# Two-layer conditional kernel: low parts and weight sums moved from GpSimd to VectorE

## The chip, the cores and the metric

One core of a Trainium2 chip runs the kernel. The metric is the device time of one execution in microseconds. The times shown are the median of three runs; the profile is that of one more execution, recorded by the hardware profiler.

## What is computed

The input x is 16 batches of 512 tokens by 512 features in f32. Each batch has a language id and an expert id.

```python
h = relu(x @ w1[language] + b1[language])                       # 512 -> 128
adapted = h @ w2[language] + b2[language]                       # 128 -> 512
x1 = x + layernorm(x + adapted) * gamma[language] + beta[language]
g = gelu(x1 @ W1 + B1)                                          # 512 -> 2048, exact gelu
out = x1 + concat([g @ W2 + B2, g @ We[expert] + be[expert]])   # 384 + 128 columns
```

## The kernel before

The batches are worked on in eight pairs. Within a pair the hidden width of 2048 is cut into eight groups (k = 0 to 7) of 2 x 128 columns. All operands of TensorE (PE) are split: a high part, rounded to the type fp32r by ScalarE (ACT), and a low part, which is the value minus its high part. Every product of two matrices is three matmuls, high by high, high by low and low by high (lines 276 to 278; line numbers are those of the profile). A 128x512 low part is one TENSOR_TENSOR subtraction on VectorE (DVE) or GpSimd (POOL).

**The up product.** For the two batches of a pair and the two halves of the inner dimension, the blocks B11, B21, B12, B22 of x1 and A11, A12, A21, A22 of the weights are multiplied in Strassen's way with seven products instead of eight, P1 to P7, into the banks up_a, up_b and up_c. The products need sums of blocks, T1 to T4 (128x512 in two halves c each), and sums of weights, S1 to S4 (128x256 each). T1 = B12 - B11, T2 = B22 - T1, T3 = B22 - B12, T4 = B21 - T2. P5 needs T1, P6 needs T2, P7 needs T3 and P4 needs T4, in the order P1, P5, P6, P2, P3, P7, P4 (`pe_step`). P2 needs B21 and P3 needs B22. VectorE makes the values of T (`dve_t1` to `dve_t4`), ScalarE rounds them (`act_t_hi`), and the low part is made by GpSimd (`pool_t_lo`, line 1362), but for T1 of the second pair, which is `dve_t_lo` (line 1029).

**The first pair.** Its weights come raw from memory. For each group k from 1 the sums S1 to S4 are made by GpSimd (`pool_weight_sums`, lines 1369 to 1377), ScalarE rounds all seven weight blocks (`act_w1_hi`, line 751) and VectorE makes their low part (`dve_w1_lo`, line 1060). Both parts are kept in device memory and loaded again by the later pairs (`keep_w1`, `load_w1`).

**The other work.** While PE works on pair i, the adapter of pair i + 1 is worked on in between: its weights are split (`act_aw_hi`, then `pool_aw_lo`, line 1284, or in one place `dve_aw_lo`, line 1073), its products go to PE (`pe_adapter_up` into aux; `pe_adapter_down` in groups 2 to 5, the first token tile into up_a, the second into up_c), and VectorE does the layer norm. The down product (`pe_down`, 24 matmuls for one batch and group) reads g from VectorE (`dve_g_lo`, line 876) and expert weights from GpSimd (`pool_expert`, lines 1356 and 1358). VectorE adds the finished banks to the output (`dve_down_sum`: eight small operations for batch 0, lines 888 and 890; four for batch 1, line 895). GpSimd also makes the residual (`pool_residual`, line 1339) and two sums per token tile of the next pair (`pool_biases`, lines 1296 and 1298).

**The order.** Each engine's order is written out by hand, by `pe_step`, `act_step`, `dve_step`, `pool_step` and `sp_pair` and their branches for the first pair. An engine takes its instructions strictly in that order and waits on semaphores. The second half of the adapter's down product may not write up_c before VectorE has read the group's P5 and P3 out of it:

```python
pe_adapter_down(eng, m, b, t, up_a)
eng.wait_ge(dve_c12, seven(i, k + 1))      # dve_sum_c12, line 866
pe_adapter_down(eng, m, b, t + 1, up_c)
```

The down product of batch 1 at a pair's end waits for the sum of batch 0 (`dve_out[0]`), and the next x may be loaded only when the T and B blocks that share its buffer have been read:

```python
if b == 0 and k < 2 and m is not pairs[1]:
    eng.wait_ge(b_low, m.count(6, 0))
    eng.wait_ge(dve_t, m.count(8, 0))      # all of T1 to T4 made
```

## Time and profile before

| | |
|---|---|
| median of 3 runs | 1426.03 us (1424.87 to 1427.23) |
| profiled execution | 1425.13 us, its span 1423.3 us |
| PE busy | 1413.5 us, 99% of the span |
| VectorE busy | 892.8 us, 63% |
| GpSimd busy | 648.2 us, 46% |
| ScalarE busy | 588.8 us, 41% |
| granted clock of PE, mean | 0.999 |

In a row of the timeline the first number is the start in us from the span's start and the second is the time from the start of the row's first instruction to the end of its last. An instruction's own duration overlaps the next one's start, so the spacing of starts is a little shorter than the duration. In brackets stands the idle time of the engine ahead of the row and what ended it. A granted clock of 1.00 is 2.4 GHz, one of 0.50 is 1.2 GHz; in a row of the windows it stands third from the end, behind the length of the stretch and the busy time of PE, its weight load, VectorE, ScalarE and GpSimd, and ahead of the DMA share and GB/s.

### The profile page before, as it was taken

What the parts mean: (1) busy time and instruction counts of PE and PEld (TensorE: products, weight loads), DVE (VectorE), ACT (ScalarE), POOL (GpSimd) and SP (SyncE); (2) the same over time, 40 slices, a digit from 0 to 9 for tenths busy, and PEclk for the clock granted to TensorE, in tenths of its full rate; (3) what the DMA queues carried; (4) which work ended last, traced back from release to release, by engine and by line L of the source; (5) the groups of instructions that cost most, each with busy time, mean ns of one, the idle gap of its engine ahead of it and who ended that gap; (6) DMA issues with size and microseconds to landing.
All of it is one profiled execution on the core that took longest, in us unless ns stands there. A gap on an engine that the chain in (4) does not pass through costs nothing.

```text
span 1423.3 us, 18598 instructions
## 1 busy us (share of the span) xinstructions
PE 1413.5 (99%) x6220; PEld 1162.7 (82%) x6220; DVE 892.8 (63%) x1457; ACT 588.8 (41%) x968; POOL 648.2 (46%) x643
## 2 busy tenths in 40 slices
PE   9999999999999999999999999999999999999999
PEld 6788878888888888888888888888888888888887
DVE  6998794765746756568566575556666576643333
ACT  4844454333543335343353434443345333533231
POOL 5996365451464424734257342563335633351101
PEclk9999999999999999999999999999999999999999
DMA  8646897457765677566774677646876458654332
GB/s 270 251 158 220 227 365 252 168 177 201 253 227 181 188 220 249 197 215 172 228 255 161 211 191 242 240 152 200 226 246 244 147 176 222 199 193 163 134 111 89
DMA packets 273955, 292.37 MB, mean 205 GB/s; under 512 B 129602, under 2 KB 230722, under 8 KB 265796
## 3 DMA queue, kind: packets, MB, share of 16 engines
q1 hardware_dynamic: 264068, 188.15, 44.3%
q10 hardware_dynamic: 9792, 103.03, 19.1%
q8 instruction: 50, 0.82, 0.2%
q14 instruction: 45, 0.37, 0.1%
HBM read 238.70 MB, written 52.43 MB: 205 GB/s over the span
## 4 chain that ended last, share of the span: by engine, by line
PE 93%; SPq 2%; DVE 2%; issue 1%; DMA 1%; POOL 1%; ACT 0%; DVEq 0%; ACTq 0%
PE down L277 16%; PE down L276 16%; PE down L278 16%; PE up_b L277 5%; PE up_b L278 5%; PE up_b L276 5%; PE up_c L277 4%; PE up_c L278 4%; PE up_c L276 4%; PE up_a L277 4%; PE up_a L278 4%; PE up_a L276 4%; SPq L1627 1%; PE aux L276 1%; PE aux L278 1%
## 5 line engine op out<-in xcount | busy, mean ns | idle before, releaser
L876 DVE TENSOR_TENSOR g<-g_raw,g 128x512 fp32r<-128x512 f32 x256 | 231.3, 932 | 280.3 <-ACT g L663 280.3
L277 PE MATMUL down<-w,g 128*128 128x512 f32 x1024 | 398.4, 389 | 0.0
L276 PE MATMUL down<-w,g 128*128 128x512 f32 x1024 | 398.4, 389 | 0.0
L278 PE MATMUL down<-w,g 128*128 128x512 f32 x1024 | 398.3, 389 | 0.0
L1356 POOL CAST w<-w_raw 128x256 fp32r<-128x256 f32 x125 | 72.1, 577 | 526.6 <-DMA w_raw<-m_we 526.6
L277 PEld LDWEIGHTS down<-w,g 128*128 128x128 f32 x1024 | 192.3, 188 | 40.0
L278 PEld LDWEIGHTS down<-w,g 128*128 128x128 f32 x1024 | 192.3, 188 | 39.9
L276 PEld LDWEIGHTS down<-w,g 128*128 128x128 f32 x1024 | 192.1, 188 | 40.0
L637 ACT COPY u<-up_b 128x512 f32<-128x512 f32 x63 | 37.1, 589 | 309.0 <-PE up_b L278 289.3
L663 ACT CAST g<-g_raw 128x512 fp32r<-128x512 f32 x256 | 159.0, 621 | 8.1
L655 ACT ACTIVATE g_raw<-u,m_b_sb 128x512 f32<-128x512 f32 x63 | 45.6, 723 | 229.5 <-PE down L278 217.2
L276 PE MATMUL up_b<-bo,w 128*128 128x512 f32 x336 | 130.8, 389 | 1.1 <-POOL bo L1362 1.1
L278 PE MATMUL up_b<-bo,w 128*128 128x512 f32 x336 | 130.7, 389 | 0.0
L277 PE MATMUL up_b<-bo,w 128*128 128x512 f32 x336 | 130.7, 389 | 0.0
L1358 POOL TENSOR_TENSOR w<-w_raw,w 128x256 fp32r<-128x256 f32 x128 | 113.2, 884 | 10.0
L895 DVE TENSOR_TENSOR resid<-down,resid 128x512 f32<-128x512 f32 x128 | 83.5, 684 | 41.8 <-PE down L278 41.8
L655 ACT ACTIVATE g_raw<-up_b,m_b_sb 128x512 f32<-128x512 f32 x63 | 43.2, 686 | 139.7 <-PE up_b L278 139.6
L1339 POOL TENSOR_TENSOR resid<-x,m_bias 128x512 f32<-128x512 f32 x64 | 89.7, 1432 | 0.0
L276 PE MATMUL up_c<-bo,w 128*128 128x512 f32 x224 | 87.1, 389 | 0.0
L277 PE MATMUL up_c<-bo,w 128*128 128x512 f32 x224 | 87.1, 389 | 0.0
L278 PE MATMUL up_c<-bo,w 128*128 128x512 f32 x224 | 87.1, 389 | 0.0
L866 DVE TENSOR_TENSOR u<-up_c,u 128x512 f32<-128x512 f32 x63 | 43.4, 689 | 62.0 <-PE up_c L278 53.9
(224 smaller groups left out, 2443.1 us busy)
## 6 DMA issues: line engine op xcount, KB each, us to landing
w<-w_kept ACTq DMA_DIRECT2D x55, 1792.0 KB, 7.6
w<-w_kept SPq DMA_DIRECT2D x56, 768.0 KB, 4.9
w_raw<-m_we SPq DMA_DIRECT2D x128, 128.0 KB, 4.6
out<-resid SPq DMA_DIRECT2D x64, 256.0 KB, 4.4
xTs_raw<-xT SPq DMA_DIRECT2D x56, 256.0 KB, 3.1
xs<-x SPq DMA_DIRECT2D x56, 256.0 KB, 6.5
w_kept<-w SPq DMA_DIRECT2D x8, 1792.0 KB, 8.9
x_turned<-turned SPq DMA_DIRECT2D x112, 128.0 KB, 3.5
```

The lines of the kernel that those rows point to most:

```text
L276: eng.matmul(bank, a_hi, b_hi, start=opens, stop=False, skip_group_check=True)
L277: eng.matmul(bank, a_hi, b_lo, start=False, stop=False, skip_group_check=True)
L278: return eng.matmul(bank, a_lo, b_hi, start=False, stop=closes, skip_group_check=True)
L637: eng.copy(u2[:, :], up_b[:, :]).then_inc(act_u2, 1)
L655: eng.activation(values, source, ACT.Gelu, bias=m_b1_sb[:, j:j + 1]).then_inc(act_gelu, 1)
L663: eng.copy(g[:, b, k % 2, h, HI, :], values).then_inc(act_ghi[b], 1)
L866: eng.tensor_tensor(u2[:, :], up_c[:, :], u2[:, :], ALU.add).then_inc(dve_c12, 1)
L876: eng.tensor_tensor(g[:, b, k % 2, h, LO, :], g_raw[:, b, k % 2, h, LO, :], raw(g[:, b, k % 2, h, HI, :]), ALU.subtract).then_inc(dve_glo[ ...
L895: eng.tensor_tensor(resid[:, 1, t, :], down[t][:, :], resid[:, 1, t, :], ALU.add).then_inc(dve_out[1], 1)
L1339: eng.tensor_tensor(resid[:, b, t, :], x1[:, b, t, :], m_bias[:, b, :], ALU.add).then_inc(pool_res, 1)
L1356: eng.tensor_copy(hi, values).then_inc(pool_eh[b], 1)
L1358: eng.tensor_tensor(lo, values, raw(hi), ALU.subtract).then_inc(pool_e[b], 1)
```

## The change

VectorE gets the weight sums of groups 2 to 7 of the first pair (`dve_weight_sums`); GpSimd keeps those of group 1 and of the group loaded again at the pair's end. VectorE gets the low parts of T2 and T3 of the first pair and of all four T of every later pair; GpSimd keeps T1 and T4 of the first pair. VectorE gets all adapter weights' low parts in later pairs, and the first of the first pair. One semaphore per T takes the place of a common one. On ScalarE the rounding of B22 goes ahead of that of T3, and T4's behind the gelu of C11. At the very start of the program PE corrects each half of B11 directly behind its first products, and ScalarE keeps each half directly behind its rounding.

```diff
+        if k in (1, GROUPS):
+            eng.wait_ge(pool_s, 4 * (1 + k // GROUPS))
+        else:
+            eng.wait_ge(dve_s, 4 * (k - 1))
         eng.copy(w1[:, k % 2, HI, :, :], w1_raw[:, k % 2, LO, :, :]).then_inc(act_w1hi, 1)
 
     def act_w2_hi(eng, k):
...
+    def dve_weight_sums(eng, k):
+
+        w, n = w1_raw[:, k % 2, LO], 4 * (k - 2)
+        eng.wait_ge(in_w1raw[k % 2], 48 * (k // 2 + 1))
+        eng.tensor_tensor(w[:, S1, :], a21[:, k % 2, :], w[:, A22, :], ALU.add).then_inc(dve_s, 1)
+        eng.tensor_tensor(w[:, S3, :], w[:, A11, :], a21[:, k % 2, :], ALU.subtract).then_inc(dve_s, 1)
+        eng.wait_ge(dve_s, n + 1)
+        eng.tensor_tensor(w[:, S2, :], w[:, S1, :], w[:, A11, :], ALU.subtract).then_inc(dve_s, 1)
+        eng.wait_ge(dve_s, n + 3)
+        eng.tensor_tensor(w[:, S4, :], w[:, A12, :], w[:, S2, :], ALU.subtract).then_inc(dve_s, 1)
+
     def dve_w1_lo(eng, k):
         eng.wait_ge(act_w1hi, k)
...
@@ -1075,6 +1091,7 @@
     def dve_second_step(eng, i, m):
 
         dve_g_lo(eng, i, 0, C11)
+        dve_weight_sums(eng, 2)
         dve_g_lo(eng, i, 0, C21)
         dve_first_t4(eng, 0)
         dve_first_t4(eng, 1)
@@ -1121,11 +1138,14 @@
             dve_g_lo(eng, i, 6, C22)
         if k == 2:
             dve_g_lo(eng, i, 0, C22)
+            dve_weight_sums(eng, 3)
             dve_sum_c12(eng, i, k)
         if k % 2 == 0:
             dve_down_sum(eng, i, 0, k - 1)
         else:
             dve_down_sum(eng, i, 1, k - 2)
+        if 2 < k < GROUPS - 1:
+            dve_weight_sums(eng, k + 1)
         if k == GROUPS - 1:
             for c in range(2):
                 dve_t1(eng, m, c)
@@ -1182,14 +1202,19 @@
     def dve_next_blocks(eng, i):
 
         for c in range(2):
-            dve_t3(eng, i, c)
+            dve_t_lo(eng, i, T2, c)
         if before(i) is first:
             for c in range(2):
                 dve_b_lo(eng, i, B21, c)
         for c in range(2):
-            dve_t4(eng, i, c)
+            dve_t3(eng, i, c)
         for c in range(2):
             dve_b_lo(eng, i, B22, c)
...
+        for c in range(2):
+            dve_t_lo(eng, i, T3, c)
+        dve_down_sum(eng, before(i), 0, GROUPS - 1)
+        for c in range(2):
+            dve_t4(eng, i, c)
 
     def dve_step(eng, i, m, k):
         if i is first:
@@ -1205,7 +1230,6 @@
             dve_g_lo(eng, before(i), GROUPS - 1, C21)
         if k == 0:
             dve_next_blocks(eng, i)
-            dve_down_sum(eng, before(i), 0, GROUPS - 1)
         if m and last:
             for c in range(2):
                 dve_b_lo(eng, m, B11, c)
@@ -1216,6 +1240,10 @@
                 b, c = ADAPTER_UP[k]
                 dve_xT_lo(eng, m, b, c)
                 dve_xT_lo(eng, m, b, c + 1)
+            if k == 2:
+                dve_aw_lo(eng, m, 1, 0)
+            if k == 4:
+                dve_aw_lo(eng, m, 1, 1)
         if k == 1 or k > 2:
             dve_g_lo(eng, i, k - 1, C12)
             dve_g_lo(eng, i, k - 1, C22)
@@ -1246,14 +1274,19 @@
         if m and k == 1:
             dve_xT_lo(eng, m, 0, 2)
             dve_xT_lo(eng, m, 0, 3)
+            dve_aw_lo(eng, m, 0, 1)
         if m and last:
             for c in range(2):
                 dve_t1(eng, m, c)
         if not (m and k in (4, 5)):
             dve_sum_c12(eng, i, k)
         dve_sum_c22(eng, i, k)
+        if k == 0:
+            for c in range(2):
+                dve_t_lo(eng, i, T4, c)
         dve_g_lo(eng, i, k, C11)
         if m and k == 0:
+            dve_aw_lo(eng, m, 0, 0)
             dve_xT_lo(eng, m, 0, 0)
             dve_xT_lo(eng, m, 0, 1)
         if k == 0:
@@ -1269,6 +1302,8 @@
             dve_turns(eng, m, 0, 0)
         if m and last:
             for c in range(2):
+                dve_t_lo(eng, m, T1, c)
+            for c in range(2):
                 dve_t2(eng, m, c)
             for c in range(2):
...
-            for of in (T1, T2):
-                for c in range(2):
-                    pool_t_lo(eng, i, of, c)
-            pool_t_lo(eng, i, T3, 0)
-            pool_aw_lo(eng, m, 0, 0)
-            pool_t_lo(eng, i, T3, 1)
+            for c in range(2):
+                pool_t_lo(eng, i, T1, c)
             return
         if k == 1:
-            pool_weight_sums(eng, 2)
             pool_t_lo(eng, i, T4, 0)
             pool_t_lo(eng, i, T4, 1)
             pool_expert(eng, i, 0, 1)
+            eng.wait_ge(aw_split, m.front(4, 1))
             pool_aw_lo(eng, m, 0, 1)
...
@@ -1447,15 +1470,6 @@
         if i is first:
             pool_first_step(eng, i, m, k)
             return
-        if k == 0:
-            pool_t_lo(eng, i, T3, 0)
-            pool_t_lo(eng, i, T3, 1)
-            if before(i) is first:
-                pool_aw_lo(eng, m, 0, 0)
-            pool_t_lo(eng, i, T4, 0)
-            pool_t_lo(eng, i, T4, 1)
-            if m and before(i) is not first:
-                pool_aw_lo(eng, m, 0, 0)
         if m:
             pool_roots(eng, m, k)
         if k % 2 == 1:
@@ -1463,33 +1477,22 @@
             pool_expert(eng, i, 1, k - 1)
         elif k > 0:
             pool_expert(eng, i, 1, k - 1)
-        if m and k == 2:
-            pool_aw_lo(eng, m, 1, 0)
         if k in (1, 2):
             for t in range(TT):
                 pool_residual(eng, i, k - 1, t)
...
@@ -1956,10 +1957,15 @@
                 dve_b_lo(eng, first, B22, c, FIRST_B22[c])
             dve_w1_lo(eng, 1)
             for c in range(2):
+                dve_t_lo(eng, first, T2, c)
+            for c in range(2):
                 dve_t3(eng, first, c, FIRST_B22[c])
+            dve_xT_lo(eng, pairs[1], 0, 0)
+            dve_aw_lo(eng, pairs[1], 0, 0)
+            dve_xT_lo(eng, pairs[1], 0, 1)
+            for c in range(2):
+                dve_t_lo(eng, first, T3, c)
             dve_w2_lo(eng, 0)
-            for c in range(2):
-                dve_xT_lo(eng, pairs[1], 0, c)
             run(eng, dve_step)
             dve_g_lo(eng, last_pair, GROUPS - 1, C21)
             dve_down_sum(eng, last_pair, 0, GROUPS - 1)
```

What is left out: the semaphores' names, the body of the sums (now the same on both engines, with the engine's own semaphore), the moved rounding on ScalarE, and GpSimd's low parts in the first pair's groups 0 and 7.

Three places show the new order. The first is VectorE in group 2 of the first pair, ahead of the sum that reads up_c (u<-up_c). Before (aw is the adapter's weight, g the gelu's output, u the sum):

```order
L1073 TENSOR_TENSOR aw<-aw_raw,aw 128x512 [waits aw_split,aw_rounded]
L876 TENSOR_TENSOR g<-g_raw,g 128x512 [waits act_ghi1]
L866 TENSOR_TENSOR u_66<-up_c,u_66 128x512 [waits act_u2,pe_p3]
L888 TENSOR_TENSOR resid<-down,resid 128x128 [waits pool_res,pe_y0]
L890 TENSOR_TENSOR resid<-down,resid 128x384
```

Now:

```order
L1089 TENSOR_TENSOR aw<-aw_raw,aw 128x512 [waits aw_split,aw_rounded]
L881 TENSOR_TENSOR g<-g_raw,g 128x512 [waits act_ghi1]
L1067 TENSOR_TENSOR w_raw<-a_73,w_raw 128x256 [waits in_w1raw_1]
L1068 TENSOR_TENSOR w_raw<-w_raw,a_73 128x256
L1070 TENSOR_TENSOR w_raw<-w_raw 128x256 [waits dve_s]
L1072 TENSOR_TENSOR w_raw<-w_raw 128x256 [waits dve_s]
L871 TENSOR_TENSOR u_66<-up_c,u_66 128x512 [waits act_u2,pe_p3]
L893 TENSOR_TENSOR resid<-down,resid 128x128 [waits pool_res,pe_y0]
```

The four weight sums of group 3 (w_raw) have come between g and the sum that reads up_c.

The second place is GpSimd in groups 1 and 2 of the first pair. Before (bo is T4's low part, w_51 an expert's, aw an adapter's, x_68 and xs the sums for the next pair, w_raw the weight sums):

```order
L1362 TENSOR_TENSOR bo<-bo_raw,bo 128x512 [waits act_thi] x2
L1358 TENSOR_TENSOR w_51<-w_raw,w_51 128x2x128 [waits act_eh0,in_e0_1]
L1284 TENSOR_TENSOR aw<-aw_raw,aw 128x512 [waits aw_rounded]
L1339 TENSOR_TENSOR resid<-x_68,m_bias 128x512 [waits in_mb0,dve_x1] x4
L1296 TENSOR_TENSOR x_68<-xs,vecs 128x512 [waits pool_res,pe_tr0,in_vec0,in_x0_0]
L1298 TENSOR_TENSOR xs<-xs,vecs 128x512 [waits pool_xb]
L1358 TENSOR_TENSOR w_51<-w_raw,w_51 128x2x128 [waits act_eh1,in_e1_0]
L1369 TENSOR_TENSOR w_raw<-a_73,w_raw 128x256 [waits in_w1raw_1]
L1371 TENSOR_TENSOR w_raw<-w_raw,a_73 128x256
L1374 TENSOR_TENSOR w_raw<-w_raw 128x256 [waits pool_s]
L1377 TENSOR_TENSOR w_raw<-w_raw 128x256 [waits pool_s]
L1296 TENSOR_TENSOR x_68<-xs,vecs 128x512 [waits in_x0_1]
```

Now:

```order
L1397 TENSOR_TENSOR bo<-bo_raw,bo 128x512 [waits act_thi] x2
L1393 TENSOR_TENSOR w_51<-w_raw,w_51 128x2x128 [waits act_eh0,in_e0_1]
L1319 TENSOR_TENSOR aw<-aw_raw,aw 128x512 [waits aw_rounded,aw_split]
L1374 TENSOR_TENSOR resid<-x_68,m_bias 128x512 [waits in_mb0,dve_x1] x4
L1331 TENSOR_TENSOR x_68<-xs,vecs 128x512 [waits pool_res,pe_tr0,in_vec0,in_x0_0]
L1333 TENSOR_TENSOR xs<-xs,vecs 128x512 [waits pool_xb]
L1393 TENSOR_TENSOR w_51<-w_raw,w_51 128x2x128 [waits act_eh1,in_e1_0]
L1331 TENSOR_TENSOR x_68<-xs,vecs 128x512 [waits in_x0_1]
L1333 TENSOR_TENSOR xs<-xs,vecs 128x512 [waits pool_xb]
L1393 TENSOR_TENSOR w_51<-w_raw,w_51 128x2x128 [waits act_eh1,in_e1_1]
```

The sums for the next pair follow each other with one expert's low part in between; the weight sums are gone.

The third place is VectorE from the first pair's end into group 0 of the second pair. Before (h_raw is T2, the first bo_raw T3, the second T4; bo<-xTs_raw the low parts of B21, then of B22; resid<-down the output sums of batch 0):

```order
L876 TENSOR_TENSOR g<-g_raw,g 128x512 [waits act_ghi0]
L1040 TENSOR_TENSOR bo_raw<-xTs_raw,b_64 128x512 [waits pe_p7,in_turned1_2]
L1040 TENSOR_TENSOR bo_raw<-xTs_raw,b_64 128x512 [waits pe_p7,in_turned1_3]
L1001 TENSOR_TENSOR bo<-xTs_raw,bo 128x512 [waits act_bhi] x2
L1056 TENSOR_TENSOR bo_raw<-xTs_raw,h_raw 128x512 [waits dve_t,pe_p4,in_turned0_2]
L1056 TENSOR_TENSOR bo_raw<-xTs_raw,h_raw 128x512 [waits dve_t,pe_p4,in_turned0_3]
L1001 TENSOR_TENSOR bo<-xTs_raw,bo 128x512 [waits act_bhi] x2
L888 TENSOR_TENSOR resid<-down,resid 128x128 [waits dve_out0,pe_y0]
L890 TENSOR_TENSOR resid<-down,resid 128x384
```

Now:

```order
L881 TENSOR_TENSOR g<-g_raw,g 128x512 [waits act_ghi0]
L1034 TENSOR_TENSOR bo<-h_raw,bo 128x512 [waits act_thi] x2
L1006 TENSOR_TENSOR bo<-xTs_raw,bo 128x512 [waits act_bhi] x2
L1045 TENSOR_TENSOR bo_raw<-xTs_raw,b_64 128x512 [waits pe_p7,in_turned1_2]
L1045 TENSOR_TENSOR bo_raw<-xTs_raw,b_64 128x512 [waits pe_p7,in_turned1_3]
L1006 TENSOR_TENSOR bo<-xTs_raw,bo 128x512 [waits act_bhi] x2
L1034 TENSOR_TENSOR bo<-bo_raw,bo 128x512 [waits act_thi] x2
L893 TENSOR_TENSOR resid<-down,resid 128x128 [waits dve_out0,pe_y0]
L895 TENSOR_TENSOR resid<-down,resid 128x384
```

T2's low part (bo<-h_raw) and T3's (bo<-bo_raw) have come in. B21's low part has moved ahead of T3, B22's ahead of the making of T4, and the eight output sums, of which the last two rows are the first, now also stand ahead of T4.

## Rows read from the trace of the kernel before

**Rows 1.** the page's engine totals: busy us, share of the span, instructions
```profile
PE 1413.5 (99%) x6220; PEld 1162.7 (82%) x6220; DVE 892.8 (63%) x1457; ACT 588.8 (41%) x968; POOL 648.2 (46%) x643
```

**Rows 2.** waits of PE, whole program: us in total, times, longest
```profile
PE up_c L339 <- DVE bo L1001: 2.6, 2, 1.5
PE up_b L276 <- POOL bo L1362: 1.1, 1, 1.1
PE aux L276 <- POOL aw L1284: 0.4, 1, 0.4
```

**Rows 3.** timeline of VectorE, 60 to 75 us: start us, us from start to end of the row
```profile
60.50 5.18 DVE L876 TENSOR_TENSOR g<-g_raw,g 128x512 fp32r<-128x512 f32 x3
72.39 1.23 DVE L876 TENSOR_TENSOR g<-g_raw,g 128x512 fp32r<-128x512 f32 x1
73.55 0.67 DVE L866 TENSOR_TENSOR u<-up_c,u 128x512 f32<-128x512 f32 x1
74.15 0.27 DVE L888 TENSOR_TENSOR resid<-down,resid 128x128 f32<-128x128 f32 x1
74.35 0.54 DVE L890 TENSOR_TENSOR resid<-down,resid 128x384 f32<-128x384 f32 x1
```

**Rows 4.** timeline of GpSimd, 61 to 78 us
```profile
61.70 6.83 POOL L1339 TENSOR_TENSOR resid<-x,m_bias 128x512 f32<-128x512 f32 x4
76.40 1.29 POOL L1296 TENSOR_TENSOR x<-xs,vecs 128x512 f32<-128x512 f32 x1
```

**Rows 5.** timeline of PE at 76 us: second half of the adapter's down product
```profile
75.96 0.39 PE L276 MATMUL up_c<-aw,h 128*128 128x512 f32 x1
```

**Rows 6.** timeline of VectorE at 119 us, of GpSimd at 120 us
```profile
119.00 0.69 DVE L866 TENSOR_TENSOR u<-up_c,u 128x512 f32<-128x512 f32 x1 [1.56 <-PE up_c L278]
...
120.49 1.29 POOL L1296 TENSOR_TENSOR x<-xs,vecs 128x512 f32<-128x512 f32 x1
```

**Rows 7.** timeline of PE, 201 to 210 us, then the clock in a stretch of it
```profile
201.31 0.99 PE L339 MATMUL up_a<-bo,w 128*128 128x512 f32 x2
202.83 0.40 PE L332 MATMUL up_c<-bo,w 128*128 128x512 f32 x1
206.38 0.80 PE L339 MATMUL up_c<-bo,w 128*128 128x512 f32 x1 [1.18 <-DVE bo L1001]
209.47 0.40 PE L276 MATMUL down<-w,g 128*128 128x512 f32 x1
...
206.00:209.00 3.00, 2.62 (x6) 2.13 (x7) 3.00 (x10) 0.00 (x0) 1.47 (x1) 0.50 0.92 372
```

**Rows 8.** timeline of VectorE, 194 to 207 us
```profile
194.86 3.48 DVE L1040 TENSOR_TENSOR bo_raw<-xTs_raw,b 128x512 f32<-128x512 f32 x2
198.26 3.48 DVE L1001 TENSOR_TENSOR bo<-xTs_raw,bo 128x512 fp32r<-128x512 f32 x2
203.97 2.36 DVE L1001 TENSOR_TENSOR bo<-xTs_raw,bo 128x512 fp32r<-128x512 f32 x2
```

**Rows 9.** timeline: the next pair's x, its DMA issue, rounding and first product
```profile
206.40 1.06 SPq L1503 DMA_DIRECT2D xTs_raw<-xT  x2
...
213.81 1.27 ACT L668 CAST xTs<-xTs_raw 128x512 fp32r<-128x512 f32 x2 [7.87 <-DMA xTs_raw<-xT]
...
219.03 0.39 PE L276 MATMUL aux<-xTs,aw 128*128 128x512 f32 x1
```

**Rows 10.** timeline of GpSimd, VectorE and PE, third pair, group 2, 418 to 430 us
```profile
421.30 5.93 POOL L1339 TENSOR_TENSOR resid<-x,m_bias 128x512 f32<-128x512 f32 x4
...
418.90 1.29 DVE L901 TENSOR_TENSOR xTs<-xTs_raw,xTs 128x512 fp32r<-128x512 f32 x2
422.76 3.33 DVE L876 TENSOR_TENSOR g<-g_raw,g 128x512 fp32r<-128x512 f32 x2
426.01 0.68 DVE L866 TENSOR_TENSOR u<-up_c,u 128x512 f32<-128x512 f32 x1
...
429.15 0.39 PE L276 MATMUL up_c<-aw,h 128*128 128x512 f32 x1
```

More of the change, by code:

```diff
@@ L813, in act_step @@
             for c in range(2):
+                act_block_hi(eng, i, B22, c)
+            for c in range(2):
                 act_t_hi(eng, i, T3, c)
-            for c in range(2):
-                act_block_hi(eng, i, B22, c)
             if before(i) is first:
@@ L1440, in pool_first_step @@
             pool_expert(eng, i, 1, k)
-            for of, c in T_ORDER[2:4]:
-                pool_t_lo(eng, m, of, c)
         elif k % 2 == 1:
@@ L1489, in pool_step @@
             pool_expert(eng, i, 1, k)
-            if m:
-                for of, c in T_ORDER[2:4]:
-                    pool_t_lo(eng, m, of, c)
     def load_xT(eng, m, b, k):
@@ L1640, in load_blocks @@
             eng.wait_ge(dve_t, m.count(8, 0))
-            eng.wait_ge(pool_tlo, m.count(8, 0))
+            eng.wait_ge(t_low[T1], m.count(2, 0))
         else:
@@ L1843, in _ @@
                 first_hi(eng, C11, A11, B11, c, c == 0)
-            for c in range(2):
                 pe_first_low(eng, B11, c, FIRST_B11[c])
@@ L1900, in _ @@
                 act_first_hi(eng, B11, c, FIRST_B11[c])
-            for c in range(2):
                 act_first_keep(eng, B11, c, FIRST_B11[c])
@@ L1958, in _ @@
             for c in range(2):
+                dve_t_lo(eng, first, T2, c)
+            for c in range(2):
                 dve_t3(eng, first, c, FIRST_B22[c])
+            dve_xT_lo(eng, pairs[1], 0, 0)
+            dve_aw_lo(eng, pairs[1], 0, 0)
+            dve_xT_lo(eng, pairs[1], 0, 1)
+            for c in range(2):
+                dve_t_lo(eng, first, T3, c)
             dve_w2_lo(eng, 0)
-            for c in range(2):
-                dve_xT_lo(eng, pairs[1], 0, c)
             run(eng, dve_step)
```

49 lines of the change are left out of this document (18 added, 31 removed).

## The prediction

> **What bounds the kernel now.** I read the engine totals first: PE is busy for 1413.5 of 1423.3 us [rows 1]. A VectorE or GpSimd instruction is therefore worth only what it makes PE wait. Next come the waits of PE; the ones that this change can touch are 2.6 us on VectorE's low part of B22, in two waits, 1.1 us on T2's low part by GpSimd and 0.4 us on an adapter weight's low part by GpSimd [rows 2]. All lie in the first pair or at the boundary to the second. So at most about 5 us are to be had, and the timelines of VectorE and GpSimd must then say whether VectorE, with more to do, comes late somewhere else.
>
> **The price of a shared stretch.** The change moves work between two engines that slow each other. Three low parts of 128x512 take 5.18 us where GpSimd is busy, 1.70 us each counted from start to start, and one takes some 0.60 alone (two in 1.29, the second's tail included) [rows 3, 10]. GpSimd's operation of the same size takes 1.29 alone and 1.70 in company (four in 6.83) [rows 4]. So where both have a queue they alternate: one of each in 1.70 us, of which 0.60 are VectorE's own and 1.10 go to GpSimd. The sum of up_c, which reads PSUM, takes 0.67 beside a busy GpSimd [rows 3] and isn't slowed. A 128x256 sum on VectorE does not occur before. By the 128- and 384-wide rows, 0.27 and 0.54 long with the tail [rows 3], I estimate 0.33 us of its own; beside a GpSimd that has a 512-wide operation ready each time it would be 0.33 + 1.10 = 1.43 us. The Trainium skill ("SBUF — State Buffer", "SBUF: two separate sides") says that the port pair is locked for a whole instruction and the other engine fully blocks: by that a sum would be 0.33 + 1.29 = 1.62. The trace is a little kinder, 1.70 where the rule would have 1.89 for a pair of 512-wide ones, and I go by the trace.
>
> **Start of the program.** T2's low part comes from VectorE right behind T2 and the 1.1 us wait goes [rows 2]; B11's corrections in another order save perhaps 0.2. But ScalarE has another rounding ahead, so P6 moves little; the adapter's wait of 0.4 goes. In all PE is about 0.5 us (0 to 1.5) earlier afterwards. It gains nothing at the end, because the next stall is set by VectorE and swallows it: 0.
>
> **Group 2 of the first pair.** The sum of up_c starts at 73.55 and ends at 74.22 [rows 3]; the second half of the adapter's down product, which waits for it, would start at 75.96 [rows 5]. Slack is 1.74 us. The change puts four weight sums ahead of this sum. VectorE also gets there about 0.5 us later, at 74.05, because of group 2's sums and two low parts earlier (estimate). GpSimd, which has residuals, the sums for the next pair and experts' low parts queued in a row, has work all through, so most of the four sums meet one of its operations. Alone they would cost 4 x 0.33 = 1.3 us, with each contended 4 x 1.43 = 5.7. Some of GpSimd's operations are only 256 wide, so I take 1.25 each, 5.0 us, near the upper end, as the g ahead of them is contended too (1.16 to the next start instead of some 0.60 [rows 3]). The sum of up_c then ends at 79.7 and PE goes on at 79.8: **+3.85** (0 to +5). Nothing follows on PE that could be taken forward: its order is strict.
>
> **The clock behind that wait.** At the pair boundary PE idled for 1.47 and 1.18 us, and then ran at a granted clock of 0.50, the 1.2 GHz level, until about 209: matmuls lasted 0.80 and not 0.39 [rows 7]. From 206.38 to 209.47 are 3.1 us, half of which is lost. A stall of almost 4 us should bring the same: **+1.5** (0 to 2).
>
> **Groups 3 to 6.** Here the sums stand behind the down product's sums. In group 4 the sum of up_c starts at 119.00 with VectorE idle for 1.56 ahead of it, and GpSimd begins its sums for the next pair beside it at 120.49 [rows 6]; those now come earlier. The sums of groups 5 and 6 are done beside them. Slack there is 1.2 us, and 4 x 1.43 = 5.7 does not fit quite: **+0.6** for both (0 to 2). In groups 3 and 6 VectorE's idle time covers them: 0. If that cover were gone, each late sum would be passed on 1 to 1.
>
> **The boundary to the second pair.** Before, VectorE made T3 (3.48 us for two), B21's low part (3.48), T4, and B22's low part at 203.97 (2.36) [rows 8]. PE needed the last at 203.05, right behind 202.83, and waited; with the clock behind it and 0.4 us for B21's low part (0.99 instead of 0.61 for two at 201.31) the down product of group 7 began at 209.47 [rows 7]. Without waits it is 204.48, 14 matmuls behind 201.31 at 0.227 us each (1413.5 / 6220 [rows 1]). Now GpSimd has nothing at this place, so VectorE runs at 0.60: T2's low part 194.9 to 196.1, B21's to 197.3, T3 to 198.5, B22's to 199.7, T3's low to 200.9. The eight output sums (0.20 and 0.46 us apart, 2.65 us [rows 3]) end at 203.5, T4 at 204.7. All stand before their use: **-5.0** (-5.3 to -4). What becomes late next: the next pair's x is loaded behind the last reader of its buffer. It was issued at 206.40 and its rounding waited 7.87 us, till 213.81, for a transfer beside full queues (DMA share 0.92 [rows 7, 9]). Its first product ran at 219.03 [rows 9] and without the 5.0 us it comes at 214.0. The issue comes only 1.6 us earlier, and the load lands no earlier, as the queues are full; rounding and low part follow, to 215.1. So **+1.0** (0 to 2) comes back.
>
> **Second to seventh pair, group 2.** This repeats six times. In the third pair the adapter's down product is at 429.15; up_c is summed at 426.01 to 426.69, with slack 2.4 [rows 10]. The change puts a low part of an adapter weight ahead (0.60 alone, 1.70 contended), and GpSimd, rid of its own, starts its four residuals (5.93 [rows 10]) earlier, so more of VectorE's operations fall beside it: one or two at 1.10 each. I get the sum's end at 429.2 against 429.15, **+0.1** each, **+0.6** (0 to +9). One more GpSimd operation in that stretch gives another 1.1 each, 6.6 in all. T1 and T2 at the pair's end, and T4 in group 0, have idle VectorE time around them: 0.
>
> **Sum.** 3.85 + 1.5 + 0.6 - 5.0 + 1.0 + 0.6 = +2.55 on the profiled execution's 1425.13, 1427.7. The median of the runs is 0.9 above that execution, so **1428.5 us**. That is within 0.2% (2.85 us, about what a measurement of this kernel can tell from no change), but near its upper edge.
>
> **Rivals.**
> - *VectorE keeps the port.* The four sums are short and follow at once, and GpSimd may not get in between. Then they cost 1.3 to 1.8 us, the stall in group 2 is 0.2 to 0.7 and the clock stays up. For it: g at 72.39 took 1.23, not 1.70 [rows 3]. Against: three g in a row alternated at 1.70. The Trainium skill (same section) gives the pair to whichever instruction starts first, which this rival would fit as well; who goes first when both wait it doesn't say. The sum becomes 0.5 + 0 + 0.2 - 5.0 + 1.0 + 0 = -3.3, 1422.7 us: faster. Chance 0.2.
> - *The wait repeats in six pairs (slower).* The adapter weight's low part in group 2 meets one more GpSimd residual than I count. The end of up_c's sum passes 429.15 by 1.1 us in each, and PE waits six times. It decides from one operation on, as the slack left is about 0. Added to the forecast it is +6.6, 1435 us. For it: 2.4 us of slack against 1.7 for the low part and 1.1 for another. Against: GpSimd may have done its residuals before VectorE's own work there begins. Chance 0.15.
> - *The boundary wait is only moved.* x's load lands or B22's rounding comes late, so that two stalls of over a microsecond stay and the clock falls again: -2 in place of -4, some 1431 us. Chance 0.13. It needs ScalarE to be late with the B22 and T3 roundings, which it now does first.
>
> **How the numbers follow.** The forecast's own case has 0.52; its unknown costs (0 to 5, 0 to 2, 0 to 2) make it 1424.5 to 1431.5. Faster by over 0.2% needs under 1423.2: the first rival. Slower needs over 1428.9: the two slow rivals, 0.28, and somewhat under half of the forecast's case, which lies just beside that edge. So 0.2, 0.35, 0.45. The range from 1421.8 to 1433.5 takes in the first rival, the third and the forecast, and leaves the second's upper part out.
>
> **What would show it.** Right: a PE wait of 3 to 4 us on up_c near 76 us, released by VectorE's sum, with the clock at 0.50 behind it; VectorE's four sums spaced about 1.25 us; no wait of L339's at 203 us, and one of about 1 us at the adapter's up product near 214. Wrong: sums at 0.33 us, or no drop of the clock behind the wait; PE waits in group 2 of later pairs; a wait at the boundary on B22 or T3.

## The result and the profile after

The changed kernel takes **1429.11 us** (median of 14 runs, 1426.26 to 1430.42), the kernel before in the same runs 1426.27 us (14 runs, 1423.56 to 1428.24). The ratio is 1.0020, with a 95% interval from 1.0012 to 1.0027: slower by 0.2%, 2.84 us by the medians. The profiled execution took 1428.87 us, its span is 1427.1, against 1425.13 and 1423.3 before.

| PE reaches the same matmul at | before | after | difference | change since the row above |
|---|---|---|---|---|
| down product, group 1 of the first pair | 63.04 | 63.13 | +0.09 | +0.09 |
| adapter's down product in up_c, group 2 | 75.96 | 79.02 | +3.06 | +2.97 |
| up product of group 3, past the slow clock | 82.08 | 86.65 | +4.57 | +1.51 |
| down product of group 7 at the pair boundary | 209.47 | 209.05 | -0.42 | -4.99 |
| adapter's up product, second pair | 219.03 | 219.95 | +0.92 | +1.34 |
| adapter's down product in up_c, second pair, group 2 | 255.07 | 257.04 | +1.97 | +1.05 |
| last matmul | 1419.68 | 1423.41 | +3.73 | +1.76 |

The table is made from the timelines of PE. The page's engine totals and the waits of PE (us in total, times, longest):

```profile
PE 1414.9 (99%) x6220; PEld 1163.5 (82%) x6220; DVE 926.3 (65%) x1564; ACT 589.9 (41%) x968; POOL 514.1 (36%) x536
...
PE up_c L277 <- DVE u L871: 3.5, 2, 2.7
...
PE up_b L277 <- ACT up_b L630: 1.5, 1, 1.5
PE aux L277 <- DVE xTs L906: 1.2, 1, 1.2
PE down L277 <- DVE g L881: 0.5, 1, 0.5
```

GpSimd has 134 us less to do than before, VectorE 33.5 us more, and PE is as full [rows 1]. The two waits on B22 and the ones on GpSimd [rows 2] are gone. In their place stand waits on VectorE's sum of up_c, on ScalarE's copy into up_b in the first pair, on x's low part and, 0.5 us, on g. VectorE in the stretch of [rows 3], where the four weight sums are the L1067 to L1072 rows and L871 is the sum of up_c:

```profile
73.16 1.51 DVE L1067 TENSOR_TENSOR w_raw<-a,w_raw 128x256 f32<-128x256 f32 x1
74.59 1.51 DVE L1068 TENSOR_TENSOR w_raw<-w_raw,a 128x256 f32<-128x256 f32 x1
76.02 0.94 DVE L1070 TENSOR_TENSOR w_raw<-w_raw 128x256 f32<-128x256 f32 x1
77.00 1.37 DVE L1072 TENSOR_TENSOR w_raw<-w_raw 128x256 f32<-128x256 f32 x1
78.29 0.68 DVE L871 TENSOR_TENSOR u<-up_c,u 128x512 f32<-128x512 f32 x1
```

GpSimd in the same stretch (compare [rows 4]), with no idle time:

```profile
72.65 1.73 POOL L1331 TENSOR_TENSOR x<-xs,vecs 128x512 f32<-128x512 f32 x1
74.46 1.35 POOL L1333 TENSOR_TENSOR xs<-xs,vecs 128x512 f32<-128x512 f32 x1
75.78 0.91 POOL L1393 TENSOR_TENSOR w<-w_raw,w 128x256 fp32r<-128x256 f32 x1
76.64 1.44 POOL L1331 TENSOR_TENSOR x<-xs,vecs 128x512 f32<-128x512 f32 x1
```

The first two sums and the fourth stand beside 512-wide operations of GpSimd, the third, the shortest, beside the 256-wide one that began at 75.78: from start to start they take 1.43, 1.43, 0.98 and 1.29 us, 5.13 in all. PE there (compare [rows 5]), and the clock behind the wait:

```profile
79.02 0.79 PE L277 MATMUL up_c<-aw,h 128*128 128x512 f32 x1 [2.69 <-DVE u L871]
80.47 0.63 PE L277 MATMUL down<-w,g 128*128 128x512 f32 x1
...
79.00:82.00 3.00, 2.98 (x7) 2.40 (x8) 3.00 (x9) 1.09 (x1) 2.92 (x3) 0.50 0.00 0
```

PE is idle for 2.69 us ahead of the needed sum's reader, and then six matmuls and more run at the granted clock of 0.50, which is 1.2 GHz. At the boundary GpSimd has no instruction from 197.7 until past 212, so VectorE is not slowed by it (compare [rows 8]):

```profile
199.19 1.30 DVE L1034 TENSOR_TENSOR bo<-h_raw,bo 128x512 fp32r<-128x512 f32 x2 [0.34 <-ACT bo L748]
200.40 1.28 DVE L1006 TENSOR_TENSOR bo<-xTs_raw,bo 128x512 fp32r<-128x512 f32 x2
201.60 1.28 DVE L1045 TENSOR_TENSOR bo_raw<-xTs_raw,b 128x512 f32<-128x512 f32 x2
202.81 1.29 DVE L1006 TENSOR_TENSOR bo<-xTs_raw,bo 128x512 fp32r<-128x512 f32 x2
204.01 1.29 DVE L1034 TENSOR_TENSOR bo<-bo_raw,bo 128x512 fp32r<-128x512 f32 x2
...
207.86 1.29 DVE L1061 TENSOR_TENSOR bo_raw<-xTs_raw,h_raw 128x512 f32<-128x512 f32 x2
```

In order: T2's low part, B21's, T3, B22's, T3's low part and, behind the output sums, T4. Ten operations take 0.60 us each where they took up to 1.70. B22's low part is done at 204.1. PE, which needed it at once before, needs it at 207.24 here:

```profile
207.24 0.62 PE L340 MATMUL up_c<-bo,w 128*128 128x512 f32 x2
...
209.05 0.39 PE L277 MATMUL down<-w,g 128*128 128x512 f32 x1
```

Behind it the next x is late (compare [rows 9]); first its DMA issue, then ScalarE, then PE:

```profile
211.26 1.02 SPq L1506 DMA_DIRECT2D xTs_raw<-xT  x2
...
218.46 1.24 ACT L669 CAST xTs<-xTs_raw 128x512 fp32r<-128x512 f32 x2 [8.65 <-DMA xTs_raw<-xT]
...
219.95 0.47 PE L277 MATMUL aux<-xTs,aw 128*128 128x512 f32 x1 [1.22 <-DVE xTs L906]
```

And this is group 2 of the third pair (compare [rows 10]):

```profile
415.89 5.50 POOL L1374 TENSOR_TENSOR resid<-x,m_bias 128x512 f32<-128x512 f32 x4
...
421.86 3.48 DVE L906 TENSOR_TENSOR xTs<-xTs_raw,xTs 128x512 fp32r<-128x512 f32 x2
425.26 1.77 DVE L1089 TENSOR_TENSOR aw<-aw_raw,aw 128x512 fp32r<-128x512 f32 x1
...
429.61 1.28 DVE L881 TENSOR_TENSOR g<-g_raw,g 128x512 fp32r<-128x512 f32 x2
430.82 0.68 DVE L871 TENSOR_TENSOR u<-up_c,u 128x512 f32<-128x512 f32 x1
...
431.54 0.50 PE L277 MATMUL up_c<-aw,h 128*128 128x512 f32 x1
```

GpSimd begins its four residuals at 415.89, 5.4 us earlier than before, since it no longer waits for the adapter weight. VectorE's two low parts of x now take 3.48 us instead of 1.29, the adapter weight's 1.77. The two g behind them are cheaper than before, 1.28 instead of 3.33, but the sum of up_c ends at 431.50, and PE, which would be there at 431.25, starts at 431.54.

### The profile page after: what moved, and what is told of

It is laid out like the page before. It is cut to its first block, busy times and chain, and to the rows that moved or that the text cites. A ratio compares the mean times of both kernels' runs of the same rounds, so it can differ in the third digit from the quotient of the medians.

```text
span 1427.1 us, 18624 instructions
## 1 busy us (share of the span) xinstructions
PE 1414.9 (99%) x6220; PEld 1163.5 (82%) x6220; DVE 926.3 (65%) x1564; ACT 589.9 (41%) x968; POOL 514.1 (36%) x536
## 4 chain that ended last, share of the span: by engine, by line
PE 87%; DVE 5%; SPq 3%; DMA 2%; issue 2%; ACT 1%; POOL 0%; DVEq 0%; ACTq 0%; POOLq 0%
PE down L279 15%; PE down L278 15%; PE down L277 15%; PE up_b L279 5%; PE up_b L278 5%; PE up_b L277 5%; PE up_c L277 4%; PE up_c L279 4%; PE up_c L278 4%; PE up_a L279 3%; PE up_a L278 3%; PE up_a L277 3%; SPq L1630 1%; DVE g L881 1%; DVE xTs L906 1%
## 5 line engine op out<-in xcount | busy, mean ns | idle before, releaser
L881 DVE TENSOR_TENSOR g<-g_raw,g 128x512 fp32r<-128x512 f32 x256 | 201.3, 815 | 273.3 <-ACT g L664 273.2
L1367 POOL TENSOR_TENSOR rstd<-var_eps,minus_half 128x1 f32<-128x1 f32 x64 | 49.9, 786 | 128.1 <-DVE var_eps L929 127.4
```

Source lines behind the costliest of these rows:

```text
L881: eng.tensor_tensor(g[:, b, k % 2, h, LO, :], g_raw[:, b, k % 2, h, LO, :], raw(g[:, b, k % 2, h, HI, :]), ALU.subtract).then_inc(dve_glo[ ...
L1367: eng.tensor_tensor(rstd[:, n - 1:n], var_eps[:, n - 1:n], minus_half[:, :], ALU.pow).then_inc(pool_rstd, 1)
```

## The experiments

Each was timed beside the kernel before; ratios are to that kernel, with 95% intervals. The changed kernel's own is 1.0020 (1.0012 to 1.0027). The kernel before has medians of 1425.8 to 1426.9 us in different groups of runs, so profiles carry the terms and the ratios the totals.

### Group 3's weight sums back on GpSimd

```diff
         if k == 2:
             dve_g_lo(eng, i, 0, C22)
-            dve_weight_sums(eng, 3)
             dve_sum_c12(eng, i, k)
...
             pool_expert(eng, i, 1, 0)
+            pool_weight_sums(eng, 3)
             pool_biases(eng, m, 0, 1)
```

The semaphores are counted accordingly.

> The changed kernel, with the four weight sums of group 3 alone back on GpSimd, where they stood before. Theory (VectorE's four contended sums ahead of up_c's sum made the 2.69 us wait at 79.02 and the clock at 0.50 behind it): the sum of up_c ends near 74.0, no PE wait at 76, clock 1.00, and the time falls by 3.0 + 1.5 = 4.5 us to about 1424.6. Rival (the wait there comes from the low parts added earlier on VectorE, and the sums only fill it): the wait stays at 1 us or more and the time falls by under 2 us.

Measured: 1426.21 us, ratio 1.0005 (0.9995 to 1.0014). The sum of up_c ends at 73.7, the wait at 76 is gone and the clock stays up; by the up product of group 3 PE is 4.52 us ahead of the changed kernel. But 1.7 us of that is lost again in group 4 of the first pair. There VectorE's sums of group 5 stand ahead of the sum of up_c as well, and meet GpSimd (VectorE, then PE):

```profile
118.72 1.51 DVE L1070 TENSOR_TENSOR w_raw<-w_raw,a 128x256 f32<-128x256 f32 x1
120.15 1.50 DVE L1072 TENSOR_TENSOR w_raw<-w_raw 128x256 f32<-128x256 f32 x1
...
122.03 0.68 DVE L873 TENSOR_TENSOR u<-up_c,u 128x512 f32<-128x512 f32 x1
...
122.77 0.50 PE L277 MATMUL up_c<-aw,h 128*128 128x512 f32 x1 [1.42 <-DVE u L873]
```

In the changed kernel this wait does not show, because PE came 4.2 us later there. The first wait **covered** the second. The theory holds for the place; the total I expected was too good by the covered wait.

### GpSimd yields to the sums

```diff
             pool_expert(eng, i, 1, 0)
+            eng.wait_ge(dve_s, 8)
             pool_biases(eng, m, 0, 1)
```

> The changed kernel; GpSimd's two sums for the next pair's second token tile (and all it does after them) wait until VectorE has made group 3's weight sums. Nothing is moved off VectorE. Theory (it is the port shared with GpSimd that makes a 256-wide sum cost 1.2 us): the four sums are spaced about 0.35 us, up_c's sum ends near 75, before PE needs it at 76.2, no wait and no clock drop, about 1424.6 us. Rival (a 256-wide sum on VectorE costs about 1 us by itself, or the waits among the sums do): spacing stays near 1 us, up_c's sum ends near 78 and the time stays at 1429.

Measured: 1425.73 us, ratio 1.0001 (0.9992 to 1.0010). VectorE:

```profile
73.15 0.41 DVE L1067 TENSOR_TENSOR w_raw<-a,w_raw 128x256 f32<-128x256 f32 x1
...
74.26 0.42 DVE L1072 TENSOR_TENSOR w_raw<-w_raw 128x256 f32<-128x256 f32 x1
74.61 0.69 DVE L871 TENSOR_TENSOR u<-up_c,u 128x512 f32<-128x512 f32 x1
```

The four sums go from 73.15 to 74.61, 1.46 us together instead of 5.13, and the sum of up_c is done at 75.3. Nothing was taken off VectorE. So the price of 1.28 us a sum is 0.37 of its own and 0.9 of GpSimd's. So it is GpSimd's work beside them that makes the sums long, and not that VectorE is slow on these. The covered wait in group 4 comes out here too, 0.98 us.

### The sums behind the sum of up_c

```diff
-            dve_weight_sums(eng, 3)
             dve_sum_c12(eng, i, k)
+            dve_weight_sums(eng, 3)
```

> The changed kernel; group 3's four weight sums stay on VectorE but stand behind up_c's sum instead of ahead of it. Theory (the sums have a second deadline: ScalarE rounds their result in 1.7 us and VectorE's low part of it takes 3.1 us, all before PE's up product at about 82.3): up_c's wait is gone, but the low part ends near 86 and PE waits 3 to 4 us on VectorE's low part of w at the up product, again with the clock at 0.50; total within 1 us of 1429. Rival (the sum of up_c was the only thing that was late): the whole 4.5 us come back, 1424.6.

Measured: 1427.23 us, ratio 1.0012 (1.0003 to 1.0021). The total lies between the two expectations, and the mechanism is neither. PE waits, but in front of the down product, for VectorE's output sums (L895), which the weight sums had pushed back:

```profile
79.00 0.47 PE L277 MATMUL down<-w,g 128*128 128x512 f32 x1 [2.17 <-DVE resid L895]
...
79.00:82.00 3.00, 3.00 (x13) 2.51 (x14) 3.00 (x8) 0.91 (x1) 2.92 (x4) 1.00 0.02 5
```

The weight's low part ended at 85.5 and cost 0.3 us at most. I had named the wrong second deadline. The clock stayed at 1.00 behind a wait of 2.17 us.

### Residuals held back in the later pairs

```diff
         if k in (1, 2):
+            if m and k == 2:
+                eng.wait_ge(aw_split, m.front(4, 3))
             for t in range(TT):
                 pool_residual(eng, i, k - 1, t)
```

> The changed kernel; in group 2 of the six later pairs GpSimd waits with its four residuals until VectorE has made the adapter weight's low part, which is about when GpSimd started them before the change. Theory (the steps of +1.05, 0.4, 0.4, 0.3 us per pair come from GpSimd starting its residuals 4 us earlier and so contending with VectorE's low parts of x, 3.48 instead of 1.29 us for two, not from the 0.6 us of the moved low part): up_c's sum ends more than 1 us before PE needs it in each pair and the time falls by 2.8 us to about 1426.3. Rival (the moved instruction itself is what is too much): the waits stay at 0.3 to 0.8 us each, no change.

Measured: 1426.45 us, ratio 1.0002 (0.9993 to 1.0011). GpSimd and VectorE in the third pair, group 2:

```profile
422.11 6.03 POOL L1374 TENSOR_TENSOR resid<-x,m_bias 128x512 f32<-128x512 f32 x4 [7.29 <-DVE aw L1089]
...
420.14 1.29 DVE L906 TENSOR_TENSOR xTs<-xTs_raw,xTs 128x512 fp32r<-128x512 f32 x2
421.35 0.68 DVE L1089 TENSOR_TENSOR aw<-aw_raw,aw 128x512 fp32r<-128x512 f32 x1
...
427.19 0.69 DVE L871 TENSOR_TENSOR u<-up_c,u 128x512 f32<-128x512 f32 x1 [0.21 <-PE up_c L279]
```

VectorE's low parts of x are back at 1.29 us, and it even idles ahead of the sum of up_c, which waits for PE (0.21 us) and not the other way round. From 90 us to the end PE gains 3.0 us on the changed kernel. The moved low part, 0.68 us, costs nothing. What cost time in the six pairs was that taking work off GpSimd let its next work start earlier, into VectorE's busy stretch.

### The language id read early

```diff
                     load_biases(eng, m, 0, language_a)
+                    if i is not first:
+                        language_b = language_of(eng, m, 1)
                     load_x(eng, m, 0)
                     load_gamma(eng, m, 0, language_a)
-                    language_b = language_of(eng, m, 1)
+                    if i is first:
+                        language_b = language_of(eng, m, 1)
```

> The changed kernel; in group 0 of the later pairs SyncE reads the language id of the second batch ahead of the loads of x instead of behind the load of gamma, so that nothing but the wait for T4 stands between gamma's load and the load of the next pair's transposed x. Theory (that load is issued at 211.26, 2.1 us behind T4's making at 209.15, because SyncE is busy reading the id; landing follows the issue by 7.2 us): issue at about 209.2, ScalarE's rounding at about 216.4 instead of 218.46, the PE wait of 1.22 at 219.95 gone, time lower by 1.2 us, about 1427.9. Rival (my prediction's: the DMA queues are full and the landing is set by them, not by the issue): rounding still at 218.4 and the wait stays.

Measured: 1429.42 us, ratio 1.0020 (1.0011 to 1.0029). The edit misfired: SyncE had issued the vector ahead at 201.35 and came to the loads of x only at 209.88, so reading the id took over 7 us there, where behind gamma it had taken under 3. The load of the transposed x was issued 2.4 us later than in the changed kernel, but ScalarE rounded it only 0.67 us later (219.13). PE waited 2.20 us for it at 220.62, against 1.22, and ran at a granted clock of 0.50 for some 3 us behind that. The run did not test its theory as meant, but it says that landing follows the issue only weakly.

### The boundary, taken apart

Four kernels undo parts of the boundary. The first puts VectorE's steps into the old order, with all low parts still on VectorE:

```diff
         for c in range(2):
             dve_t_lo(eng, i, T2, c)
+        for c in range(2):
+            dve_t3(eng, i, c)
         if before(i) is first:
             for c in range(2):
                 dve_b_lo(eng, i, B21, c)
         for c in range(2):
-            dve_t3(eng, i, c)
+            dve_t4(eng, i, c)
         for c in range(2):
             dve_b_lo(eng, i, B22, c)
         for c in range(2):
             dve_t_lo(eng, i, T3, c)
         dve_down_sum(eng, before(i), 0, GROUPS - 1)
-        for c in range(2):
-            dve_t4(eng, i, c)
```

> The changed kernel with VectorE's boundary steps in the order of before (T3, B21's low part, T4, B22's low part, then T3's low part and the output sums), all low parts still on VectorE. Theory (the 5.0 us at the boundary come from VectorE running at 0.60 us an operation since GpSimd is silent; the new order is not needed): B22's low part ends by 205.3, T3's by 206.5, before PE needs them at 207.2 and 208.6; no wait on them; the output sums end about 209.1, costing 0 to 0.3 at the down product; total within 0.5 us of 1429.1. Rival (the order of the two B blocks is what gave the gain): waits of 1 us or more at 207 come back, with the clock at 0.50 behind them, +2 to +5.

Measured: 1428.66 us, ratio 1.0014 (1.0005 to 1.0022), with no wait at 207. The second keeps the new order and returns T2's and T3's low parts to GpSimd (`dve_t_lo` out of `dve_next_blocks`, `pool_t_lo` for T2 at a pair's end and for T3 in group 0):

> The changed kernel with the low parts of T2 and T3 of the second and later pairs back on GpSimd, where they stood, but the new order on VectorE. Theory (contention sets the pace at the boundary): VectorE's operations beside them take 1.7 us instead of 0.60 each, B22's low part ends near 206.5 and T3's near 208.5, so up to 2 us of waits return at up_c or up_b near 207 to 209. Rival (the new order alone is enough): no wait on the low parts of B or T at the boundary, same time as the changed kernel.

Measured: 1428.85 us, ratio 1.0015 (1.0006 to 1.0023). No wait either: VectorE's operations took 1.15 us each, not the 1.7 that I had put into the expectation, since GpSimd idled for 1.28 us between T2's and T3's low parts, and B22's low part ended at 207.5, while PE came to its first half at 208.96. The third undoes both at once:

> The changed kernel with both parts of the boundary undone at once: T2's and T3's low parts on GpSimd in the second and later pairs, and VectorE's steps there in the order of before. Theory (order and engine are two remedies for the same wait, and either is enough; with neither it returns): VectorE's B22 low part is the last of five pairs of operations, four of them contended at 1.1 to 1.7 us each, and ends 1 to 3 us behind PE's need; PE waits twice on it in up_c near 207 with the clock at 0.50 behind, +3 to +5 us over the changed kernel, about 1433, less 1.2 if x's wait vanishes. Rival (ScalarE's new order, B22's rounding ahead of T3's, is what removed it): no wait on B22, 1429.

Measured: 1428.91 us, ratio 1.0018 (1.0009 to 1.0027). My theory failed: PE loses only 0.9 us at the boundary, the clock does not fall, and x's wait is gone (-1.38). The fourth adds T4 as it was, rounded early and its low part on GpSimd:

> The kernel with the old order and T2's and T3's low parts on GpSimd, and in addition T4 as before: rounded by ScalarE directly behind T3, its low part made by GpSimd. Theory (what was left of the boundary's gain there is that GpSimd had fallen silent when VectorE made B22's low part, 1.28 us for two instead of 2.36): B22's low part takes about 2.4 us again and ends 1.1 us later, PE's wait on it in up_c grows from 0.9 us in all to about 2 us in two waits, and the clock may fall to 0.50 behind them; +1 to +3 us over that kernel, less what the wait for x hides. Rival (ScalarE's rounding of B22 ahead of T3's was the rest): B22's low part is as early as there and the time the same, 1429.

Measured: 1429.35 us, ratio 1.0023 (1.0014 to 1.0033). B22's low part in the third kernel and in the fourth, then the waits of PE of the fourth:

```profile
207.34 1.28 DVE L1006 TENSOR_TENSOR bo<-xTs_raw,bo 128x512 fp32r<-128x512 f32 x2
```

```profile
208.03 2.36 DVE L1008 TENSOR_TENSOR bo<-xTs_raw,bo 128x512 fp32r<-128x512 f32 x2
...
PE up_c L340 <- DVE bo L1008: 1.6, 2, 1.2
...
PE up_a L340 <- DVE bo L1008: 0.5, 1, 0.5
```

T4's low part beside it makes it 2.36 us instead of 1.28 (the making of T4 became as much shorter and that of T3 as much longer, as GpSimd's low parts fell beside other operations), and all waits of before are there again, in the same places: 1.6 and 0.5 us against 2.6 [rows 2] and the 0.4 that [rows 7] show in up_a. From the g ahead of T3 to the end of B22's low part it is 12.1 us before, 11.0 in the fourth kernel, 9.9 in the third, 7.6 with the low parts on GpSimd alone, 5.9 in the change; PE needs its first half by 9.1 (207.24 less 198.17 in the change). The 1.1 us between the first two are the making of T4, 2.38 before and 1.28 in the fourth kernel, where GpSimd no longer has an adapter weight's low part beside it. So the gain has no single cause: several moves each shorten the same chain by 1 to 3 us, and the change makes more of them than it needs.

None of this shows in the totals: the four ratios, 1.0014 to 1.0023, can't be told from the change's 1.0020. The profile of the fourth kernel says why. Against the change PE loses 2.9 us at the boundary, but it gets 1.4 back where the change waits for x, and another 1.4 by group 2 of the third pair, ahead of the adapter's down product. In this execution it then loses 0.3 to 0.5 us again at each of three such places (477, 607 and 956 us). What the boundary gains, later waits take back in part or in whole: they had been covered.

### The holds together, and x first

Three holds on GpSimd (in groups 1 and 4 of the first pair behind the weight sums, and the residuals of the later pairs):

```diff
+            eng.wait_ge(dve_s, 8)
             pool_biases(eng, m, 0, 1)
...
+            eng.wait_ge(dve_s, 16)
             pool_biases(eng, m, 1, 1)
...
+            if m and k == 2:
+                eng.wait_ge(aw_split, m.front(4, 3))
             for t in range(TT):
```

The first version had the early reading of the language id as well:

> The changed kernel with four waits or moves together: GpSimd holds its sums for the next pair back until VectorE has made the weight sums, in groups 1 and 4 of the first pair; it holds its residuals back in group 2 of the later pairs; SyncE reads the language id early. Theory: first pair's wait -4.5, later pairs -2.8 to -3.0, x's wait -1.2, and no new wait of 1 us in group 4: 1429.1 - 8.5 = 1420.6, faster than both kernels by about 0.4%. Rival (the waits cover one another, as group 4's wait of 1.0 to 1.4 appeared once group 2's was gone): 2 to 3 us of it are taken back elsewhere, 1423.

Measured: 1422.49 us, ratio 0.9967 (0.9954 to 0.9980). One wait of 0.90 us was left in the fourth pair: the adapter weight had been loaded late, and VectorE, which now makes its low part, stood behind it for 3.73 us:

```profile
594.96 0.69 DVE L1089 TENSOR_TENSOR aw<-aw_raw,aw 128x512 fp32r<-128x512 f32 x1 [3.73 <-ACT aw L690]
```

Without that edit:

> The changed kernel with only the three holds on GpSimd: behind the weight sums in groups 1 and 4 of the first pair, and behind the adapter weight's low part in group 2 of the later pairs; SyncE as in the changed kernel. Theory (the early reading of the language id did nothing for x and made an adapter weight land late, at 594.96 in the fourth pair, 0.9 us of PE's time): the first pair's 4.4 and the later pairs' 3.0 us come back, no wait at 601, x's wait of about 1 us stays: 1421.7, 0.3% faster than before. Rival: the wait in the fourth pair is the holds' own and stays, 1422.5.

Measured: 1422.36 us, ratio 0.9974 (0.9964 to 0.9984). No wait on the sum of up_c is left anywhere, in the first pair or later. Of the changed kernel's others there remain x's, 0.9 us, and those at the start, 1.5 us on up_b and 0.5 us on g. Last, the old order on VectorE again (T4 is made early) and x issued first:

```diff
                     load_biases(eng, m, 0, language_a)
+                    if i is not first:
+                        load_xT_pair(eng, m, 0, 0)
                     load_x(eng, m, 0)
...
             if i is not first and k == 0:
-                load_xT_pair(eng, m, 0, 0)
                 store(eng, before(i), 0)
```

> The kernel with the three holds, VectorE's boundary steps in the order of before (T4 is then made about 204 less the 4.4 us) and the next pair's transposed x issued ahead of the four loads of x instead of behind them. Theory (the landing of x at the boundary is set by what stands ahead of it in the DMA queues, four loads of 256 KB among it): it lands 3 us or more before 214, the PE wait of 1.1 us at the adapter's up product goes, 1420.5. Rival (ordering within the queues is worth nothing, or the loads of x, now 1 to 2 us later, become late themselves): no gain over the kernel with the holds alone.

Measured: 1421.58 us, ratio 0.9964 (0.9952 to 0.9976). ScalarE's rounding of x in this kernel, and in the one with the holds alone:

```profile
211.95 1.27 ACT L669 CAST xTs<-xTs_raw 128x512 fp32r<-128x512 f32 x2 [5.99 <-DMA xTs_raw<-xT]
```

```profile
214.65 1.26 ACT L669 CAST xTs<-xTs_raw 128x512 fp32r<-128x512 f32 x2 [8.34 <-DMA xTs_raw<-xT]
```

It is 2.7 us earlier and the PE wait of 0.9 us is gone. The load was issued 4.4 us earlier (202.41 against 206.83) and also ahead of the four loads of x; no run separates the two. The old order alone, in the first kernel of the boundary, issued it 0.85 us earlier than the change and had it rounded at 218.51, no earlier. PE gains 1.1 us at this place on the kernel with the holds alone, and gives them back: 0.7 us in group 2 of the second pair, where it waits 0.54 us for the sum of up_c, and the rest by the fourth pair. So this lead, too, is lost in a wait that had been covered, and the two totals can't be told apart (the intervals overlap). By its median this is the fastest kernel of the study: 0.36% faster than before, 0.5% faster than the change.

## Why the prediction was right, point by point

I forecast 1428.5 us and the kernel takes 1429.11. The sum was +2.55; measured are +2.84 by the medians and +3.74 by the profiled executions (1428.87 less 1425.13), whose parts follow. That the total fits better than its parts is in part luck: group 2 and groups 3 to 6 were together 1.5 us too high, x and the later pairs 2.5 too low.

- **Start of the program, 0.** T2's wait on GpSimd went and came back as one on ScalarE's copy into up_b, 1.53 us; PE was 0.59 us earlier at 48.85 and had lost it by 63.13. Right.
- **Group 2 of the first pair, +3.85.** Measured +2.97. The four sums took 5.13 us where I took 5.0. What was off is when VectorE gets there: I put it 0.5 us later than before, it was 0.4 us earlier (73.16). The experiment with GpSimd yielding shows the mechanism: it is GpSimd's work beside the sums. The wait came out under the 3 to 4 us that I had named as the sign.
- **The clock, +1.5.** Measured +1.51 in this execution, of which some 0.2 come with the wait itself, as they do where the clock stays up. That it agreed is luck in part: see below.
- **Groups 3 to 6, +0.6.** Measured 0, because the wait ahead covered it. It is there, 1.42 and 0.98 us, as soon as the first is removed. The term was real and should not have been added to the first one: a later deadline counts only from where PE arrives.
- **The boundary, -5.0.** Measured -4.99 at this place, with VectorE at 0.60 us an operation. But my reading that all of it comes from GpSimd's silence is too narrow: with T2's and T3's low parts on GpSimd again the waits stay away as long as the order is new, and with the old order too PE loses only 0.9 us of the gain, as long as T4's low part is not on GpSimd. And to the end of the program the gain is worth less, since it uncovers later waits.
- **x at the boundary, +1.0.** Measured +1.34. The issue did not come 1.6 us earlier: with the 4.57 us of the first pair taken off it came 0.3 us later (211.26 against 206.40), 2.1 us behind the making of T4, and the rounding was as late as forecast. That the landing follows the issue only weakly is borne out: issued 2.4 us later it was rounded 0.67 later. Issued 4.4 us earlier, and ahead of four other loads, it came 2.7 us earlier.
- **Group 2 of the later pairs, +0.6.** Measured +2.8 (1.05 in the second pair, the rest in the other five). **This is the term that was mis-sized.** I counted one or two contended operations more and let the sum of up_c end just on time. Four were contended (h, two low parts of x, the adapter weight's), since GpSimd started 5.4 us earlier, and only the two g behind them became cheaper. The slower rival named this very mechanism and priced it at 6.6; it was real and between the two, and the hold on the residuals takes it away whole. PE waits in group 2 of the later pairs, which I had listed as a sign of being wrong, did appear, 0.80 us in the second pair.

The first rival, VectorE keeping the port, is refuted: sums of 0.37 us alternated with GpSimd's operations all the same. The third, waits at the boundary that only move, did not come. (I had reckoned it from -4, where my sum has -5.0; and the stated range leaves the second rival's 1435 out whole, not only its upper part.) The Trainium skill ("SBUF — State Buffer", "SBUF: two separate sides") has the port pair locked for a whole instruction. The trace agrees in kind, and in size it stays a little kinder: two VectorE sums beside GpSimd's 512-wide ones took 1.43 us each, where 0.37 + 1.29 would be 1.66.

## What to carry to other kernels

When two engines share a port, moving an instruction from one to the other changes two schedules: the receiver does more, and the giver's next work starts earlier, often just beside the receiver's. Look where the giver's queue goes next, and if it has slack let it wait on purpose; here three waits on GpSimd turned 0.2% lost into 0.3% gained. Waits on one strict queue cover one another, so add them up in the order of time, each from where the engine then is.
